# Two of eight gate spreads moved from TensorE and ScalarE to transfers through DRAM, in a fused window-attention and mixture-of-experts kernel

## The reference, cut to what matters

```python
t = _to_tokens(x)                                     # (4, 16384, 64)
def _L0_ffn_ref(x, ...):                              # x is the layer-normalised t
    router_probs = softmax(x @ router_w + router_b)
    top_p, top_i = top_k(router_probs, 2)
    top_p = top_p / sum(top_p)
    expert_out = einsum('bnd,edc->bnec', x, expert_w) + expert_b
    gathered = take_along_axis(expert_out, top_i[..., None], axis=2)
    return einsum('bnk,bnkc->bnc', top_p, gathered)
t = t + _L0_ffn_ref(_ln_t(t), ...)
```

## Time and profile before

| | |
|---|---|
| median of 3 runs | 1373.47 us (1370.99 to 1375.1) |
| the profiled execution's own time | 1371.55 us |
| its span, first to last instruction | 1369.8 us |
| mean granted TensorE clock | 0.985 |
| busy: TensorE, VectorE, ScalarE, GpSimd | 91%, 85%, 64%, 64% of the span |
| `g_t` copies (one for each group) | 64, from 119.9 to 1355.2 us |

### The profile page before, as it was taken

How to read it: one execution, slowest core, us unless ns; L and a number is a source line. 1 busy time by engine, 2 the same in 40 slices (tenths; PEclk the granted TensorE clock), 3 DMA queues, 4 the chain that set the end, 5 groups by cost and what they waited for, 6 DMA issues and landing times.

```text
span 1369.8 us, 47545 instructions
## 1 busy us (share of the span) xinstructions
PE 1246.1 (91%) x19840; PEld 785.7 (57%) x19840; DVE 1162.3 (85%) x2476; ACT 880.8 (64%) x1617; POOL 882.2 (64%) x758
## 2 busy tenths in 40 slices
PE   4378999988999999998999999999899999999986
PEld 3266666555666656655555666665566656666542
DVE  7737889988888898998898899899888888888874
ACT  5356767766666767766666777775666666666632
POOL 0245777865766777785667678776666676766632
PEclk9989999999999999999999999999999999999998
DMA  6002423321222333332122333432222222222221
GB/s 179 16 11 65 96 65 89 89 63 36 66 66 46 92 88 75 79 72 65 42 59 64 75 80 87 95 67 49 64 54 55 61 62 65 55 53 65 58 65 39
DMA packets 95552, 91.52 MB, mean 67 GB/s; under 512 B 26797, under 2 KB 62253, under 8 KB 95342
## 3 DMA queue, kind: packets, MB, share of 16 engines
q1 hardware_dynamic: 95342, 88.49, 27.9%
HBM read 36.03 MB, written 17.83 MB: 39 GB/s over the span
## 4 chain that ended last, share of the span: by engine, by line
PE 55%; DVE 21%; ACT 9%; issue 7%; DMA 5%; POOL 1%; SPq 1%; DVEq 0%; POOLq 0%; ACTq 0%
PE bank_y L521 12%; PE bank_s L405 8%; PE bank_s L379 6%; DVE t_g L977 6%; PE bank_t L420 5%; PE bank_o L433 4%; PE bank_p L448 4%; PE bank_e L477 3%; ACT k_m L640 3%; DVE mx L869 3%; DVE x L891 3%; PE bank_o L460 2%; PE bank_g L510 2%; DMA r_b<-recip_rows 2%; PE bank_p L510 2%
## 5 line engine op out<-in xcount | busy, mean ns | idle before, releaser
L1069 POOL TENSOR_TENSOR prob<-prob,mx 128x512 f32<-128x512 f32 x256 | 261.5, 1043 | 92.4 <-DVE mx L869 92.2
L521 PE MATMUL bank_y<-t_g,w_exp 128*64 128x512 f32 x1024 | 281.5, 626 | 18.7 <-DVE t_g L977 13.7
L1091 POOL TENSOR_TENSOR t_g<-t_t,g_copy 128x512 f32<-128x512 f32 x128 | 165.6, 1293 | 151.5 <-ACT g_copy L692 151.2
L660 ACT ACTIVATE prob<-prob 128x512 f32<-128x512 f32 x256 | 160.8, 628 | 150.3 <-POOL prob L1069 148.7
L664 ACT ACTIVATE prob_t<-bank_t 128x512 f32<-128x512 f32 x256 | 152.3, 595 | 139.9 <-PE bank_t L420 139.7
L1081 POOL TENSOR_TENSOR ln<-ln,mhalf 128x8 f32<-128x8 f32 x64 | 105.0, 1640 | 158.2 <-DVE ln L905 158.2
L420 PEld LDWEIGHTS bank_t<-idn,prob 128*128 128x128 f32 x1024 | 111.2, 144 | 137.4 <-issue 103.5
L862 DVE TENSOR_TENSOR prob<-bank_s,rel 128x1024 f32<-128x1024 f32 x128 | 156.6, 1223 | 36.2 <-PE bank_s L405 31.1
L420 PE MATMUL bank_t<-idn,prob 128*128 128x128 f32 x1024 | 169.5, 289 | 17.6 <-ACT prob_t L664 10.4
L977 DVE TENSOR_TENSOR t_g<-t_t,bank_p 128x512 f32<-128x512 f32 x256 | 174.2, 680 | 6.0 <-PE bank_p L510 5.9
L405 PEld LDWEIGHTS bank_s<-k_m,q_t 32*64 32x64 f32 x4096 | 114.5, 135 | 72.2 <-issue 68.8
(11 more groups left out here) (111 smaller groups left out, 2398.2 us busy)
## 6 DMA issues: line engine op xcount, KB each, us to landing
t_t<-t_rout SPq DMA_DIRECT2D x256, 128.0 KB, 3.7
x_in<-in_x SPq DMA_DIRECT2D x68, 256.0 KB, 3.8
r_b<-recip_rows SPq DMA_DIRECT2D x64, 256.0 KB
out_y<-y_out SPq DMA_DIRECT2D x128, 128.0 KB, 2.5
r_in<-sum_b SPq DMA_DIRECT2D x64, 16.0 KB
recip_rows<-r_out SPq DMA_DIRECT2D x64, 16.0 KB, 1.4
gate_sel<-in_sel SPq DMA_DIRECT2D x1, 512.0 KB
rel<-in_relb SPq DMA_DIRECT2D x1, 256.0 KB
```

What stands on the lines that cost most here:

```text
L521: mm(B_Y[C * a:C * a + C, :], w_exp[:, pair, :], t_g[:, (2 * pair + a) % TG, :], start=False, stop=(pair == MIXES // 2 - 1), skip_group_ch ...
L660: A(prob[:, i], prob[:, i], ACT.Exp).then_inc(p_ready.sem, 1)
L1069: G.tensor_tensor(sc, sc, mx[:, i, :].unsqueeze(2).broadcast_to([P, 2 * HEADS, NTOK]), ALU.subtract).then_inc(s_shifted.sem, 1)
L1091: G.tensor_tensor(t_g[:, u % TG, :], t_t[:, p, u % 2, :], g_copy[:, n % 2, :], ALU.mult).then_inc(tg_pool.sem, 1)
```

## The change

`ON_POOL` becomes (4, 5), both units of expert pair 2. Their gates no longer pass through L510 and L692. Step 15 of the routing writes the gates to SBUF (`g_f`), TensorE turns them as f32 once more (one more transpose in `turn_gates`), ScalarE copies these 64 rows to `g_rows` ahead of `g_t`, SyncE writes them to DRAM (`gate_rows`) and then reads each unit's two rows back, spread over 64 partitions each, into `g_copy`. GpSimd takes units 4 and 5 one behind the other after `normalise_input`, and both wait for both spreads. TensorE issues the gate matmuls of units 6 and 7 ahead of `project_out`. SyncE waits until `r_b` has landed before it issues the four `t_t` transfers.

```diff
-ON_POOL = (2, 6)
+ON_POOL = (4, 5)
+        g_f = sb("g_f", [P, ROWS * EXPERTS])
+        g_rows = sb("g_rows", [ROWS * EXPERTS, P])
+        gate_rows = nc.dram_tensor("gate_rows", [2, EXPERTS, 4, P], F32).ap()
...
+            def keep_gates(g):
+                sp.wait_ge(rows_ready.sem, rows_ready.at(g, 1))
+                if g:
+                    sp.wait_ge(g_spread.sem, g_spread.at(g))
+                sp.dma_start(gate_rows.rearrange("a e k t -> k a e t"), g_rows[:, :]).then_inc(rows_kept.sem, 16)
+
+            def spread_gates(g):
+                sp.wait_ge(rows_kept.sem, rows_kept.at(g, 16))
+                if g:
+                    sp.wait_ge(tg_pool.sem, tg_pool.at(g))
+                for n, u in enumerate(ON_POOL):
+                    first = u // 2 * 2
+                    src = gate_rows[u % 2, first:first + 2].rearrange("e k t -> e (k t)")
+                    sp.dma_start(g_copy[:, n, :], src.unsqueeze(1).broadcast_to([2, C, BANK])).then_inc(g_spread.sem, 16)
...
                 if outputting:
                     spread_reciprocals(j - 1)
+                if mixing:
+                    keep_gates(j - 3)
+                if outputting:
+                    spread_rows(j - 1)
+                if mixing:
+                    spread_gates(j - 3)
                 if routing_on:
+                    if outputting:
+                        sp.wait_ge(recip_spread.sem, recip_spread.at(j - 1, 16))
                     spread_tokens(j - 2, p)
...
                 for k in range(4):
-                    last = tr(gt16[:, k * P:(k + 1) * P], g3[:, k].rearrange("p a e -> p (a e)"), idn16[:, :])
+                    tr(gt16[:, k * P:(k + 1) * P], g3[:, k].rearrange("p a e -> p (a e)"), idn16[:, :])
+                last = tr(B_G[0:ROWS * EXPERTS, BANK // 2:BANK // 2 + P], g_f[:, :], idn[:, :])
...
-                if mixing:
-                    gates(j - 3, 4)
...
                 if mixing:
-                    gates(j - 3, 5)
                     gates(j - 3, 6)
+                    gates(j - 3, 7)
                 if outputting:
                     project_out(j - 1)
-                if mixing:
-                    gates(j - 3, 7)
...
                 act.wait_ge(gt_done.sem, gt_done.at(g, 1))
+                A(g_rows[:, :], B_G[0:ROWS * EXPERTS, BANK // 2:BANK // 2 + P], ACT.Copy).then_inc(rows_ready.sem, 1)
                 A(g_t[:, :], B_G[:, :].bitcast(BF16)[:, 0:BANK], ACT.Copy).then_inc(gt_ready.sem, 1)
...
-                if mixing:
-                    copy_gates(j - 3, 2)
...
-                if mixing:
-                    copy_gates(j - 3, 6)
...
                 if mixing:
+                    gate(j - 3, 1 - p, 2)
                     gate(j - 3, 1 - p, 3)
-                    gate(j - 3, 1 - p, 4)
...
                 if mixing:
-                    gate(j - 3, 1 - p, 5)
+                    gate(j - 3, 1 - p, 6)
...
-                pool.wait_ge(g_copied.sem, g_copied.at(g, n + 1))
+                pool.wait_ge(g_spread.sem, g_spread.at(g, 32))
...
-                if mixing:
-                    gate(j - 3, 1 - p, 2)
...
                 if mixing:
-                    gate(j - 3, 1 - p, 6)
+                    gate(j - 3, 1 - p, 4)
+                    gate(j - 3, 1 - p, 5)
```

More of the change, by code:

```diff
@@ L222, in build @@
         gt_ready = sem("gt_ready")
-        gate_done = sem("gate_done", MIXES)
-        g_copied = sem("g_copied", len(ON_POOL))
+        rows_ready = sem("rows_ready")
+        rows_kept = sem("rows_kept", 16)
+        gate_done = sem("gate_done", len(ON_DVE))
+        g_spread = sem("g_spread", 32)
         tg_dve = sem("tg_dve", MIXES - len(ON_POOL), primed=1)
@@ L301, in spread_reciprocals, with spread_rows @@
                 sp.dma_start(recip_rows.rearrange("a (c x) -> (a c) x", x=CHUNK), r_out[:, :]).then_inc(recip_kept.sem, 16)
+            def spread_rows(g):
                 sp.wait_ge(recip_kept.sem, recip_kept.at(g, 16))
@@ L505, in gates @@
                     pe.wait_ge(sum_copied.sem, sum_copied.at(min(g + 2, LAST) if isinstance(g, int) else g + 2, 1))
-                elif u and u - 2 in ON_POOL:
-                    pe.wait_ge(g_copied.sem, g_copied.at(g, ON_POOL.index(u - 2) + 1))
                 elif u:
-                    pe.wait_ge(tg_dve.sem, tg_dve.at(g, ON_DVE.index(u - 2) + 1))
+                    pe.wait_ge(tg_dve.sem, tg_dve.at(g, ON_DVE.index(u) - 1))
                 mm(B_GATE[u % 2][:, :], gate_sel16[:, u, :], g_t[:, :], start=True, stop=True).then_inc(gate_done.sem, 1)
@@ L687, in copy_turned_gates @@
                 act.wait_ge(gt_done.sem, gt_done.at(g, 1))
+                A(g_rows[:, :], B_G[0:ROWS * EXPERTS, BANK // 2:BANK // 2 + P], ACT.Copy).then_inc(rows_ready.sem, 1)
                 A(g_t[:, :], B_G[:, :].bitcast(BF16)[:, 0:BANK], ACT.Copy).then_inc(gt_ready.sem, 1)
-            def copy_gates(g, u):
-                act.wait_ge(gate_done.sem, gate_done.at(g, u + 1))
-                A(g_copy[:, ON_POOL.index(u) % 2, :], B_G[:, :], ACT.Copy).then_inc(g_copied.sem, 1)
             def copy_result(g):
@@ L911, in routing @@
             def routing(g, first_step, last_step):
-                logits, lg, lead, hot, rest, gates = (
-                    B_E[:, n * ROUTE_AT:(n + 1) * ROUTE_AT].rearrange("p (r e) -> p r e", e=EXPERTS) for n in range(6))
+                logits, lg, lead, hot, rest = (
+                    B_E[:, n * ROUTE_AT:(n + 1) * ROUTE_AT].rearrange("p (r e) -> p r e", e=EXPERTS) for n in range(5))
+                gates = g_f[:, :].rearrange("p (r e) -> p r e", e=EXPERTS)
                 def thrice(v, n):
@@ L972, in gate @@
             def gate(g, p, u):
-                dve.wait_ge(gate_done.sem, gate_done.at(g, u + 1))
+                dve.wait_ge(gate_done.sem, gate_done.at(g, ON_DVE.index(u) + 1))
                 if u == 0:
```

## The result

The changed kernel takes 1960.22 us (median, 1950.18 to 1963.68), against 1372.9 us for the kernel before, run beside it: a ratio of 1.4265, 95% interval 1.4208 to 1.4323, so 43% slower. Predicted were 1990 us, with a range of 1800 to 2180. The profiled execution took 1961.52 us, with a span of 1959.7 and a mean granted clock of 0.844 (0.985 before).

The account below looks back on a forecast made before the run. Instruction chains set the pace; GpSimd's gates would wait for spreads on two DMA engines. A slot of 26.7 us plus 2.5 for TensorE's clock, times 63, plus 119.9 before and 26 after, gave 1990 us; range 1800 to 2180.

Parts of the forecast that it names:

- The mechanism: Both spreads have two source rows, so share the same two DMA engines: 11.4 us together, with GpSimd's gates waiting each slot.
- the wait that puts t_t behind r_b: On SyncE: not on the path, since t_t is needed only in the next slot.
- r_b's share of 0.50 for eight rows: DMA share while r_b runs alone, read as one engine per source row, eight of 16, at 23 GB/s each.
- g_t to recip_rows: From the last g_t copy to the issue of the reciprocals' write to DRAM: 0.72 us.
- recip_rows to r_b: On SyncE, issue of the reciprocals' write 0.32 plus the wait for its landing 1.54: 1.86 us.
- r_b's issue to the gates: DMA start-up 1.39 us, r_b's own bytes 1.4 and the two spreads 11.4, before GpSimd's gates start.
- two gates: GpSimd's two gates, both behind both spreads: 2.57 us.
- from there to the next g_t, clock included: Expert pair 2 to the next g_t 7.4 us, plus 2.5 for TensorE at half speed after its wait.
- Rival 3: Each spread on two different engines, both running together: 1455 to 1630 us, say 1540; chance 0.07.
- Turning and other slots: Slots that turn x and those that do not were to take the same 29.2 us.
- The mean clock: TensorE's granted clock, 0.50 behind each wait, was put at some 0.75 in the mean.
- Rivals 1 and 2: Spreads use many engines: 1366 us (chance 0.03), or 1368 to 1385 with turning slots and late copies costing time (0.05).

Follow-up runs that it names:

- e2: The changed kernel with a third spread of the same form, to a buffer nobody reads, that GpSimd also waits for: 2313.26 us.
- e3: The changed kernel without SyncE's wait for r_b ahead of the four t_t transfers: 1970.68 us.
- e1: The changed kernel with its two spreads made four transfers of one gate row to 64 partitions each, on 16 engines: 1399.41 us.
- e4: The changed kernel with 32 idle matmuls on TensorE ahead of expert pair 2, to keep it busy through the wait: 1888.42 us.
- e11: The kernel before, units 2 and 6 kept on GpSimd, only unit 6's gate rows spread through DRAM on 16 engines: 1372.73 us, ratio 0.9983.
- e9: The changed kernel with its spreads as two 256 KB transfers of outermost dimension 64, without an added wait of t_t: 1415.25 us.
- e5: The kernel before with two added spreads a slot, to a tile nobody reads, awaited only a slot later: 1403.75 us, ratio 1.0201.

## Why the prediction was right, and where its terms were off

**The mechanism** held in every step. The spreads run on two engines (share 0.13 at 49 GB/s against the expected 0.13 at 46, for 8.4 us a slot against "about 8"), the two share them (e2), GpSimd's gates wait once a slot for the DMA of g_copy (9.6 us against "8 to 9"), TensorE stands 7.7 us against "some 8", and the wait that puts t_t behind r_b costs nothing (e3). The forecast rested on one reading, r_b's share of 0.50 for eight rows, and e1 shows that this reading was worth 561 us. VectorE waited for r_b once in the changed kernel, for 0.6 us, as expected of a transfer that stands ahead of the spreads. The cause of the slowdown is the form of the two transfers, not that the gates go through DRAM.

**The sum** for one slot, against means over 59 slots of the changed kernel:

| term | predicted | measured |
|---|---|---|
| g_t to recip_rows | 0.72 | 0.46 |
| recip_rows to r_b | 1.86 | 1.86 |
| r_b's issue to the gates | 14.2 | 14.48 |
| two gates | 2.57 | 2.48 |
| from there to the next g_t, clock included | 7.4 + 2.5 = 9.9 | 9.65 |
| slot | 29.2 | 28.94 |

The first is mostly the g_t copy standing 0.17 us later, behind the g_rows copy; counted from the start of g_rows it is 0.63. The last holds the clock: at full clock the rest of the slot takes 7.75 (e4), so the term is 1.8 to 1.9 where 2.5 was taken, in the lower part of its bounds of 1.7 to 3.4; the rest of the slot was taken a little too short in return (7.4 where it is 7.75), and the spreads 0.3 too short. That the sum came out within 0.3 us is thus in part luck: the terms' errors have opposite signs. Rival 3's lower price is off in itself, 21 x 63 + 146 + 4 = 1473 and not 1455; nothing hangs on it. Over the span: 118.9 us to the first g_t, 63 intervals of 28.8, and 25.4 behind the last, against 119.9, 29.2 and 26.

**Turning and other slots** were to be equal. Worked out from the g_t starts, 23 slots that turn x have a mean of 29.26 us and the 36 others 28.73: nearly so, and the half microsecond between them was not followed up. The landing of the reciprocals' write moves a slot by more (29.96 and 27.94 us above). **The mean clock** was given as some 0.75 and was 0.844. A deficit of 0.156 over a slot of 28.8 us is 9.0 us at half speed, 4.4 of them behind the gates; so TensorE kept its full clock for part of the idle stretch as well, which the rough figure had not allowed.

**What was wrong** is the estimate for 16 engines. Rivals 1 and 2 gave 1366 to 1385, and e1 gives 1399. They held that copies landing 6.4 us behind r_b's issue would be in time; in e1 the gates start 6.43 behind it in the mean, and GpSimd, which has no gate of unit 2 ahead of normalise_input any more, is there earlier and waits in 46 groups (in the slot shown it is done at 1064.40, 3.5 us behind r_b's issue, and waits 2.32), while pair 1 waits for two late gates. Both together had been put at 7 us and "a few late ones". e11, which has neither, is level with the kernel before; but it also spreads half the bytes, and its turning slots are longer as well (20.32 us against 20.07, the others 19.51 against 19.56), without any pairing. So that these two together make up the loss of e1 is the best reading of its waits, not a thing shown.

## What to carry to other kernels

Before a transfer is put on a path, see how many DMA engines it gets: the share in a window where it runs alone tells it, and here the rewriting of a 2 x 64 source as four transfers of 64 turned 1960 us into 1399. A work split that makes one consumer need two late results can cost even when the engines' totals don't change (here by the waits of e1, not by a run of its own), so look at the pairs when you choose which unit goes to which engine. And a long wait in the profile is worth only the distance to the next one behind it: e11 took away 88 us of them and gained 2.5.

## What the runs showed of the hardware that was not expected

- The load of x, which stands behind t_t in SyncE's queue, landed 9.3 us after its issue in the changed kernel and 3.8 before; it was needed two slots later, so this cost nothing. The page of each kernel, first after, then before:

```profile
x_in<-in_x SPq DMA_DIRECT2D x68, 256.0 KB, 9.3
```

```profile
x_in<-in_x SPq DMA_DIRECT2D x68, 256.0 KB, 3.8
```

- A small write to DRAM (16 KB, the reciprocals) lands 1.4 us after its issue in 44 of 64 groups of the kernel before and 43 of the changed one, and in the others after 1.7 to 3.6 us; what decides was not found. In a kernel whose slot hangs on it, this moves a slot: r_b was issued 3.02 and 1.44 us behind the write in the two slots shown.
- Two transfers of 256 KB land 0.4 us later than four of 128 KB with the same rows and engines (e9 against e1), which costs 1%.
- Transfers whose data nothing waits for in the slot still cost 26 us, 2%, and made another small transfer land 0.6 us later (e5).
